# Per-sample mixed 3x3 convolution: the input scaling of pairs 2 to 15 is done by VectorE, ahead of its statistics of the next pair, instead of by ScalarE

## The chip, the core and the metric

The kernel runs on one core of one Trainium2 chip. The metric is the device time of one launch in microseconds (us), as the median of the runs shown.

## What is computed

The input x is a batch of 32 images of 64 channels and 56x56 pixels, float32. The reference, cut to what matters:

```python
xn = group_norm(x, G=32)                      # two channels share mean and variance
pooled = xn.mean(axis=(2, 3))                 # [32, 64]
a   = relu(pooled @ fc1_w.T + fc1_b)          # K = 4 hidden values per image
att = softmax(a @ fc2_w.T + fc2_b)            # 4 mixing weights per image
agg_w = einsum('bk,koihw->boihw', att, weight)  # an own 3x3 kernel for every image
agg_b = att @ bias
out = x + conv3x3(xn, agg_w, padding=1) + agg_b
```

So every image first needs its statistics, then its own mixture of four weight sets, and only then its convolution.

## The kernel before

**Tiles.** Two images make a pair (PAIRS = 16), 64 channels each on 64 of the 128 partitions; a pair's input is one tile `x` of 128x3136 float32 in a ring of four. The convolution is made of float16 products: the scaled input and the mixed weights are each split into a high and a low float16 part (`xh`, `xl`, `wh`, `wl`), and TensorE adds high x high, low weights x high inputs (`xh,wl`) and high weights x low inputs (`xl,wh`) in PSUM. Each pair has four groups g = 0 to 3 of 14 output rows, and in each group the three products take 36 matmuls each: nine taps for the two images and the two halves of a picture. Line numbers below are those of the kernel before.

**The stages of a pair p, and who does them.**
- VectorE (DVE) takes `bn_stats` of the input in seven chunks (L321), aggregates them and swaps neighbouring channels (L329, L333), and signals `s_mv`.
- GpSimd (POOL) makes the group statistics from them, seventeen instructions on 128x1 or 128x4 operands in a chain (`group_stats`, L281 to L297). Its sixteenth, L296, signals `s_sums`; its last, L297, signals `s_norm`: the scale `xsc` and the offset `xof` of the pair are then ready.
- TensorE (PE) waits for `s_sums` and sums over channels with two small matmuls (`image_sums`, L643, output `tiny`). From pair 2 on, the sums of pair p+2 stand in TensorE's program behind group 2 of pair p; the sums of pairs 2 and 3 stand in pair 1, those of pair 2 behind group 1's `xh,wl` products and those of pair 3 behind group 2.
- ScalarE (ACT) copies them to `hid` (L559); VectorE makes `logit` and its maximum `nmax` (`logits`, L378 to L382); ScalarE takes the exponential `ex` (L570); VectorE mixes the weights (`mixture`, from `exsum` in L386 over `mix` in L400 and L402 to L410).
- ScalarE scales the input in place (`normalise`, L520: x becomes x*xsc + xof, half a picture at a time, signalled by `s_xn`) and rounds it to `xh` (`high_inputs`, L527); VectorE subtracts to get `xl` (`low_inputs`, L455) and makes `wl` (L446); ScalarE makes `wh` (L541).
- `params` (L463 to L468) makes the scale and offset of the results, ScalarE applies them to PSUM (`results`, L581), and SyncE (SP) stores.

**Order.** Nothing is scheduled by a tool: each engine runs its own list in the order in which it is written, and semaphores tie the lists together. Up to pair 1 the order is written out step by step. After that VectorE's loop over p does, in this order, the statistics of pair p+2, then logits, mixture, low inputs, low weights and params of pair p+1, while TensorE convolves pair p. ScalarE's loop does the last results of pair p-1, then `hidden`, scaling, rounding and exponentials of pair p+1, then the results of pair p. SyncE's queue loads the input of pair p+4 once the low inputs of pair p are made.

Of the kernel before, what the change touches and what calls it, by code (L numbers as in the profile page):

```python
# [39 lines left out]
X_RING = 4  # L40
# [6 lines left out]
def dynamic_conv(nc, x, w_t, small, out):  # L47
    fp32, fp16 = mybir.dt.float32, mybir.dt.float16
    ACT, AX = mybir.ActivationFunctionType, mybir.AxisListType
# [5 lines left out]
    with ctx:  # L55
        def sb(name, shape, dt=fp32):
            return ctx.enter_context(nc.sbuf_tensor(name, shape, dt))
# [4 lines left out]
        def sem(name):  # L62
            return ctx.enter_context(nc.semaphore(name))


        x_sb = [sb(f"x{i}", [P, PIX]) for i in range(X_RING)]
# [46 lines left out]
        xsc = [sb(f"xsc{i}", [P, 1]) for i in range(2)]  # L113
        xof = [sb(f"xof{i}", [P, 1]) for i in range(2)]
# [27 lines left out]
        s_norm = sem("s_norm")  # L142
# [9 lines left out]
        s_xn = sem("s_xn")  # L152
# [9 lines left out]
        def rows_of(t, half):  # L162
            return t[:, half * HALF:(half + 1) * HALF]
# [141 lines left out]
        def _(dve):  # L305
            LINKS = 8

            def link(n, ins):
                ins.then_inc(dch, 1)
                dve.wait_ge(dch, n)  # L310
# [138 lines left out]
            def low_inputs(p, half):  # L449
# [3 lines left out]
                if p >= 2:  # L453
                    dve.wait_ge(s_conv, 2 * GROUPS * (p - 1))
                nc.vector.tensor_tensor(rows_of(xl[i], half), rows_of(x_sb[p % X_RING], half),  # L455
                                        rows_of(xh[i], half), ALU.subtract).then_inc(s_xl, 1)

            def params(p):
                n, i = LINKS * p, p % 2
                if p >= 2:  # L460

                    dve.wait_ge(s_res, 2 * GROUPS * (p - 1))
                nc.vector.tensor_scalar(par[i][:, 0:1], hid[:, RANGE:RANGE + 1], 1.0 / (WLIMIT * XSCALE), None,  # L463
                                        ALU.mult)
                nc.vector.reciprocal(rsum[:], exsum[:]).then_inc(dch, 1)
                link(n + 7, nc.vector.tensor_tensor(bprod[:], ex[:], small_sb[:, BIAS:BIAS + K], ALU.mult))
                link(n + 8, nc.vector.tensor_reduce(bsum[:], bprod[:], AX.X, ALU.add))
                nc.vector.tensor_scalar(par[i][:, 1:2], bsum[:], rsum[:], gm[i][:], ALU.mult,  # L468
                                        ALU.add).then_inc(s_par, 1)
# [23 lines left out]
            low_inputs(1, 0)  # L493
            low_inputs(1, 1)
            params(1)
            for p in range(1, PAIRS - 1):
                if p + 2 < PAIRS:
                    chunk_stats(p + 2)
                    channel_means(p + 2)
                logits(p + 1)  # L500
                mixture(p + 1)
                low_inputs(p + 1, 0)
                low_weights(p + 1)
                low_inputs(p + 1, 1)
                params(p + 1)


            i, n = last_pair % 2, GROUPS * PAIRS - 1
# [5 lines left out]
        @block.scalar  # L514
        def _(act):
            def normalise(p, half):
                i = p % 2
                act.wait_ge(s_norm, p + 1)
                v = rows_of(x_sb[p % X_RING], half)
                nc.scalar.activation(v, v, ACT.Identity, bias=xof[i][:], scale=xsc[i][:]).then_inc(s_xn, 1)  # L520

            def high_inputs(p, half):
                i = p % 2
                act.wait_ge(s_xn, 2 * p + half + 1)
                if p >= 2:
                    act.wait_ge(s_conv, 2 * GROUPS * (p - 1))
                nc.scalar.activation(rows_of(xh[i], half), rows_of(x_sb[p % X_RING], half),  # L527
                                     ACT.Copy).then_inc(s_xh, 1)

            def high_from_x(p, half):  # L530
                act.wait_ge(s_norm, p + 1)
                nc.scalar.activation(rows_of(xh[p], half), rows_of(x_sb[p], half), ACT.Identity,  # L532
                                     bias=xof[p][:], scale=xsc[p][:]).then_inc(s_xh, 1)

            def high_weights(p):
                i = p % 2
                act.wait_ge(s_mix, p + 1)
                act.wait_ge(s_wsc, p + 1)
                if p >= 2:
                    act.wait_ge(s_conv, 2 * GROUPS * (p - 1))  # L540
                nc.scalar.activation(wh[i][:], mix[:], ACT.Copy, scale=wsc[i][:]).then_inc(s_wh, 1)  # L541

            def first_high_weights(n):
                if n == 0:
                    act.wait_ge(s_mix, 1)
                    act.wait_ge(s_wsc, 1)
                else:
                    act.wait_ge(s_part, 2 * K)
                part = PARTS[n]
                nc.scalar.activation(wh[0][:, part], mix[:, part], ACT.Copy, scale=wsc[0][:]).then_inc(s_wh, 1)  # L550

            def hidden(p):
                act.wait_ge(s_fc1, 2 * (p + 1))
                if p >= 1:
                    act.wait_ge(s_par, p)

                columns = slice(0, K + 1) if p == 0 else slice(0, SUMS)
                for m in range(2):
                    nc.scalar.activation(hid[halves[m], columns], tiny[m][halves[m], columns],  # L559
                                         ACT.Copy).then_inc(s_hid, 1)  # L560

            def first_range():
                act.wait_ge(s_range, 2)
                for m in range(2):
                    nc.scalar.activation(hid[halves[m], RANGE:RANGE + 1], tiny[m][halves[m], RANGE:RANGE + 1],
                                         ACT.Copy).then_inc(s_hid, 1)

            def exponentials(p):
                act.wait_ge(s_logit, p + 1)
                nc.scalar.activation(ex[:], logit[:], ACT.Exp, bias=nmax[:]).then_inc(s_exp, 1)  # L570

            def results(p, g, images=range(2)):
                i, n = p % 2, GROUPS * p + g
                for m in images:
                    if g == 0:
                        if m == 0:
                            act.wait_ge(s_outp[i], 64 * (p // 2 + 1))
                        if p >= 2:
                            act.wait_ge(stored[i][m], 48 * (p // 2))
                    act.wait_ge(s_conv, 2 * n + m + 1)  # L580
                    nc.scalar.activation(o_sb[i][m][:, g * GN:(g + 1) * GN], acc[n % SLOTS][m][:, 0:GN], ACT.Identity,  # L581
                                         bias=out_par[i][m][:, 1:2], scale=out_par[i][m][:, 0:1]).then_inc(s_res, 1)

            act.dma_start(small_sb[:], small).then_inc(s_small, 16)
            act.wait_ge(s_warm, 1)
            nc.scalar.activation(warm[:], warm[:], ACT.Exp)
            hidden(0)
            exponentials(0)
            high_from_x(0, 0)
            first_range()  # L590
            high_from_x(0, 1)
            first_high_weights(0)
            act.wait_ge(s_xh, 2)
            normalise(0, 0)
            first_high_weights(1)
            normalise(0, 1)
            results(0, 0)
            hidden(1)
            results(0, 1, (0,))
            exponentials(1)  # L600
            results(0, 1, (1,))
            high_from_x(1, 0)
            high_from_x(1, 1)
            high_weights(1)
            results(0, 2)
            act.wait_ge(s_xh, 4)
            normalise(1, 0)
            normalise(1, 1)
            for p in range(1, PAIRS):
                results(p - 1, 3)  # L610
                if p + 1 < PAIRS:
                    hidden(p + 1)
                    normalise(p + 1, 0)
                    high_inputs(p + 1, 0)
                    normalise(p + 1, 1)
                    exponentials(p + 1)
                    high_inputs(p + 1, 1)
                    results(p, 0)
                    high_weights(p + 1)
                    results(p, 1)  # L620
                    results(p, 2)
                else:
                    for g in range(GROUPS - 1):
                        results(p, g)
                    results(p, GROUPS - 1, (0,))
                    act.wait_ge(s_res_last, 1)
                    for r in range(2):
                        first = r * HALF + BANDS[r][GROUPS - 1] * GN
                        act.dma_start(out_d[2 * p + 1, :, first:first + GN],
                                      o_sb[p % 2][1][halves[r], HALF - GN:HALF]).then_inc(stored[p % 2][1], 16)  # L630
# [151 lines left out]
```

## Time and profile before

| | before |
|---|---|
| median of 3 runs | 323.12 us (322.63 to 326.03) |
| the profiled execution | 323.93 us, its span 322.1 us |
| PE busy | 301.2 us (94% of the span) |
| DVE busy | 215.6 us (67%) |
| ACT busy | 198.2 us (62%) |
| POOL busy | 75.4 us (23%) |
| the chain that ended last | PE 82%, DVE 8%, POOL 4% |

The span runs from the first to the last instruction; the execution's own time is 1.8 us more. A row of the timeline gives a start and a duration in us, the engine, the line, the operation with output and inputs, how many instructions the row joins, and in brackets how long the engine sat idle before it and which instruction released it. Idle time on an engine that nobody waits for costs nothing.

### The profile page before, as it was taken

The page shows a single profiled execution, that of the slowest core. Times are in us where ns is not written, and L with a number is a line of the kernel's source. Part 1 is how long each engine was busy: PE and PEld are TensorE (multiplying, and loading weights), DVE is VectorE, ACT ScalarE, POOL GpSimd, SP SyncE. Part 2 cuts the span into 40 slices and gives each one's busy share as a digit, 9 for nine tenths or more (in the row PEclk, how much of TensorE's full clock was granted, in tenths as well). Part 3 has the DMA queues.
Part 4 walks back from the last instruction along what each step waited for, and adds up shares of the span by engine and source line. Part 5 has one row for each costly group of instructions (what it writes and reads, how often), then busy time and mean ns, then how long its engine had stood idle before and what let it go on. Part 6 is the DMA issues. An engine that isn't in the chain of part 4 may idle for free.

```text
span 322.1 us, 15578 instructions
## 1 busy us (share of the span) xinstructions
PE 301.2 (94%) x7038; PEld 265.2 (82%) x7038; DVE 215.6 (67%) x505; ACT 198.2 (62%) x260; POOL 75.4 (23%) x268
## 2 busy tenths in 40 slices
PE   7289877999899999999999999999999999999994
PEld 5157756988679999988999899967998799988883
DVE  2899584979569494948769494949678594719000
ACT  1090776786484849567684849486675849395321
POOL 1008266028310405040220404050311305000000
PEclk9769995999999999999999999999999999999999
DMA  7962306738392947648292947668392607051464
GB/s 260 421 268 65 141 2 150 254 86 286 77 275 93 228 177 176 227 112 288 51 258 111 239 166 184 218 136 273 84 293 56 180 2 205 2 147 60 118 171 119
DMA packets 16690, 53.61 MB, mean 166 GB/s; under 512 B 7280, under 2 KB 10352, under 8 KB 14704
## 3 DMA queue, kind: packets, MB, share of 16 engines
q1 hardware_dynamic: 16320, 52.40, 54.1%
q8 instruction: 55, 0.90, 1.1%
q10 hardware_dynamic: 304, 0.22, 0.3%
q14 instruction: 11, 0.09, 0.1%
HBM read 26.89 MB, written 25.69 MB: 163 GB/s over the span
## 4 chain that ended last, share of the span: by engine, by line
PE 82%; DVE 8%; POOL 4%; DMA 2%; issue 2%; ACT 0%; SPq 0%; POOLq 0%; DVEq 0%
PE acc L674 82%; DMA x<-x 2%; DVE stats L321 2%; DVE mix L402 2%; POOL var L285 1%; DVE wparts L337 1%; POOL vsum L281 1%; PE tiny L643 0%; DVE wl L446 0%; POOL root L286 0%; DVE mix L400 0%; DVE mv L329 0%; SPq L205 0%; POOL newton L287 0%; DVE o L511 0%
## 5 line engine op out<-in xcount | busy, mean ns | idle before, releaser
L581 ACT ACTIVATE o<-acc,out_par 128x392 f32<-128x392 f32 x127 | 78.9, 670 | 78.8 <-PE acc L674 78.4
L674 PE MATMUL acc<-xl,wh 64*64 64x385 f16 (+3 forms) x2304 | 119.8, 330 | 1.4 <-issue 1.4
L674 PE MATMUL acc<-xh,wh 64*64 64x385 f16 (+3 forms) x2304 | 118.1, 326 | 1.2 <-ACT wh L550 0.5
L674 PE MATMUL acc<-xh,wl 64*64 64x385 f16 (+3 forms) x2304 | 117.4, 325 | 0.6 <-issue 0.6
L674 PEld LDWEIGHTS acc<-xl,wh 64*64 64x64 f16 x2304 | 94.4, 109 | 11.4 <-issue 1.8
L674 PEld LDWEIGHTS acc<-xh,wl 64*64 64x64 f16 x2304 | 91.3, 107 | 11.3 <-issue 1.1
L674 PEld LDWEIGHTS acc<-xh,wh 64*64 64x64 f16 x2304 | 90.8, 108 | 11.9 <-ACT xh L532 0.9
L321 DVE BATCH_NORM_STATS2 stats<-x 128x6 f32<-128x448 f32 x112 | 60.8, 612 | 6.1 <-DMA x<-x 6.1
L455 DVE TENSOR_TENSOR xl<-x,xh 128x1568 f16<-128x1568 f32 x31 | 55.3, 1785 | 0.8 <-ACT x L520 0.8
L520 ACT ACTIVATE x<-x,xof,xsc 128x1568 f32<-128x1568 f32 x32 | 53.8, 1686 | 0.4
L527 ACT ACTIVATE xh<-x 128x1568 f16<-128x1568 f32 x28 | 42.0, 1502 | 0.4
L386 DVE TENSOR_REDUCE exsum<-ex 128x1 f32<-128x4 f32 x16 | 2.5, 156 | 58.2 <-ACT ex L570 58.2
L281 POOL TENSOR_TENSOR vsum<-mv,mv_other 128x1 f32<-128x1 f32 x15 | 4.3, 289 | 158.5 <-DVE mv_other L333 158.5
L402 DVE SCALAR_TENSOR_TENSOR mix<-w_sb,ex,mix 128x576 f32<-128x576 f32 (+2 forms) x51 | 40.0, 783 | 1.8
L541 ACT ACTIVATE wh<-mix,wsc 128x576 f16<-128x576 f32 x15 | 11.6, 776 | 19.6 <-DVE mix L410 19.6
L559 ACT ACTIVATE hid<-tiny 64x6 f32<-64x6 f32 (+1 forms) x32 | 5.3, 166 | 18.7 <-PE tiny L643 18.3
L643 PEld LDWEIGHTS tiny<-sums,ones 64*64 64x64 f32 x64 | 5.5, 142 | 13.2 <-DVE sums L364 7.6
L643 PE MATMUL tiny<-sums,ones 64*64 64x6 f32 (+1 forms) x64 | 5.2, 194 | 11.8 <-DVE sums L364 7.4
L511 DVE TENSOR_SCALAR o<-acc,out_par 128x392 f32<-128x392 f32 x1 | 0.7, 684 | 20.3 <-PE acc L674 20.3
L446 DVE SCALAR_TENSOR_TENSOR wl<-mix,wsc,wh 128x576 f16<-128x576 f32 x16 | 13.0, 811 | 0.0
L656 PE MATMUL acc<-ones 128*128 128x256 f16 x58 | 10.8, 368 | 1.1 <-POOL eye L237 1.1
L656 PEld LDWEIGHTS acc<-ones 128*128 128x128 f16 x58 | 7.3, 130 | 3.5 <-POOL eye L237 1.1
(71 smaller groups left out, 146.3 us busy)
## 6 DMA issues: line engine op xcount, KB each, us to landing
x<-x SPq DMA_DIRECT2D x15, 1568.0 KB, 9.8
out<-o SPq DMA_DIRECT2D x30, 392.0 KB, 4.5
out<-o SPq DMA_DIRECT2D x30, 294.0 KB, 4.1
out<-o SPq DMA_DIRECT2D x44, 98.0 KB, 2.8
w_sb<-w_t SPq DMA_DIRECT2D x2, 576.0 KB, 8.7
out_par<-par SPq DMA_DIRECT2D x64, 0.5 KB, 2.1
x<-x SPq DMA_DIRECT2D x1, 896.0 KB, 7.1
x<-x SPq DMA_DIRECT2D x1, 448.0 KB, 3.7
```

The source lines that it names most:

```text
L281: tt(vsum[:], mv[:, 1:2], mv_other[:, 1:2], ALU.add)
L321: ins = nc.vector.bn_stats(stats[:, t, :], x_sb[p % X_RING][:, t * CHUNK:(t + 1) * CHUNK])
L402: ins = nc.vector.scalar_tensor_tensor(**share, scalar=ex[:, k:k + 1], in1=mix[:, part], op0=ALU.mult, op1=ALU.add)
L446: nc.vector.scalar_tensor_tensor(out=wl[i][:], in0=mix[:], scalar=wsc[i][:], in1=wh[i][:], op0=ALU.mult, op1=ALU.subtract).then_inc(s_wl, 1)
L455: nc.vector.tensor_tensor(rows_of(xl[i], half), rows_of(x_sb[p % X_RING], half), rows_of(xh[i], half), ALU.subtract).then_inc(s_xl, 1)
L520: nc.scalar.activation(v, v, ACT.Identity, bias=xof[i][:], scale=xsc[i][:]).then_inc(s_xn, 1)
L527: nc.scalar.activation(rows_of(xh[i], half), rows_of(x_sb[p % X_RING], half), ACT.Copy).then_inc(s_xh, 1)
L541: nc.scalar.activation(wh[i][:], mix[:], ACT.Copy, scale=wsc[i][:]).then_inc(s_wh, 1)
L581: nc.scalar.activation(o_sb[i][m][:, g * GN:(g + 1) * GN], acc[n % SLOTS][m][:, 0:GN], ACT.Identity, bias=out_par[i][m][:, 1:2], scale=out ...
L643: nc.tensor.matmul(tiny[m][halves[m], columns], ones[halves[m], 0:C], sums[halves[m], columns], start=True, stop=True).then_inc(s_fc1, 1)
L656: nc.tensor.matmul(acc[SLOTS - 1][0][:, 0:2 * P], ones[:].bitcast(fp16)[:, 0:P], ones[:].bitcast(fp16), start=True, stop=True)
L674: ins = nc.tensor.matmul(pixels[:, top:bottom, left:right], weights[i][halves[m], tap * C:(tap + 1) * C], window, start=start and step == ...
```

## The change

VectorE gets a function `normalise` that does the same in-place scaling with `tensor_scalar`, and calls it at the head of its loop for pair p+1 (so for pairs 2 to 15), before the statistics of pair p+2. ScalarE's loop no longer does it; ScalarE still scales pairs 0 and 1.

```diff
--- before.py
+++ after.py
@@ -455,6 +455,12 @@
+            def normalise(p, half):
+                i = p % 2
+                dve.wait_ge(s_norm, p + 1)
+                v = rows_of(x_sb[p % X_RING], half)
+                nc.vector.tensor_scalar(v, v, xsc[i][:], xof[i][:], ALU.mult, ALU.add).then_inc(s_xn, 1)
+
             def params(p):
@@ -494,6 +500,8 @@
             for p in range(1, PAIRS - 1):
+                for half in range(2):
+                    normalise(p + 1, half)
                 if p + 2 < PAIRS:
                     chunk_stats(p + 2)
                     channel_means(p + 2)
@@ -514,10 +522,9 @@
             def normalise(p, half):
-                i = p % 2
                 act.wait_ge(s_norm, p + 1)
-                v = rows_of(x_sb[p % X_RING], half)
-                nc.scalar.activation(v, v, ACT.Identity, bias=xof[i][:], scale=xsc[i][:]).then_inc(s_xn, 1)
+                v = rows_of(x_sb[p], half)
+                nc.scalar.activation(v, v, ACT.Identity, bias=xof[p][:], scale=xsc[p][:]).then_inc(s_xn, 1)
@@ -610,9 +617,7 @@
                 if p + 1 < PAIRS:
                     hidden(p + 1)
-                    normalise(p + 1, 0)
                     high_inputs(p + 1, 0)
-                    normalise(p + 1, 1)
                     exponentials(p + 1)
                     high_inputs(p + 1, 1)
```

On VectorE, at the first pass of its loop (p = 1), between the params of pair 1 and the exponential sum of pair 2, the order before is:

```order
L468 TENSOR_SCALAR par1<-bsum,rsum,gm1 128x1
L321 BN_STATS stats<-x3 128x6 x7
L329 BN_AGGR mv<-stats 128x2
L333 STREAM_SHUFFLE mv_other<-mv 128x2
L378 SCALAR_TENSOR_TENSOR prod<-hid,small_sb 128x20
L381 TENSOR_REDUCE logit<-prod 128x4
L382 TENSOR_REDUCE nmax<-logit 128x1
L386 TENSOR_REDUCE exsum<-ex 128x1
```

and after the change, where L474 is the old L468 and L462 is the new scaling:

```order
L474 TENSOR_SCALAR par1<-bsum,rsum,gm1 128x1
L462 TENSOR_SCALAR x2<-x2,xsc0,xof0 128x1568 x2
L321 BN_STATS stats<-x3 128x6 x7
L329 BN_AGGR mv<-stats 128x2
L333 STREAM_SHUFFLE mv_other<-mv 128x2
L378 SCALAR_TENSOR_TENSOR prod<-hid,small_sb 128x20
L381 TENSOR_REDUCE logit<-prod 128x4
L382 TENSOR_REDUCE nmax<-logit 128x1
L386 TENSOR_REDUCE exsum<-ex 128x1
```

Two scalings of pair 2, which need `s_norm` of pair 2, now stand in front of the statistics of pair 3, and the logits of pair 2 behind both. The other thirteen passes change in the same way.

On ScalarE, at the same pass, after `hidden` of pair 2, the order before is:

```order
L559 ACTIVATE hid<-tiny1 64x6
L520 ACTIVATE x2<-x2,xof0,xsc0 128x1568
L527 ACTIVATE xh0<-x2 128x1568
L520 ACTIVATE x2<-x2,xof0,xsc0 128x1568
L570 ACTIVATE ex<-logit,nmax 128x4
L527 ACTIVATE xh0<-x2 128x1568
```

and after the change, with L566, L534 and L577 for the old L559, L527 and L570:

```order
L566 ACTIVATE hid<-tiny1 64x6
L534 ACTIVATE xh0<-x2 128x1568
L577 ACTIVATE ex<-logit,nmax 128x4
L534 ACTIVATE xh0<-x2 128x1568
```

The exponential of a pair now has one rounding ahead of it behind `hidden`, where it had two scalings and a rounding.

## Rows read from the trace of the kernel before

**Rows 1.** The page: shares of the chain that ended last, by engine.
```profile
PE 82%; DVE 8%; POOL 4%; DMA 2%; issue 2%; ACT 0%; SPq 0%; POOLq 0%; DVEq 0%
```

**Rows 2.** Windows: length, then busy us (instructions) of each engine, granted clock, DMA share, GB/s.
```profile
158.00:176.00 18.00, 18.00 (x448) 17.46 (x443) 13.33 (x31) 12.43 (x17) 4.03 (x17) 1.00 0.62 183
```

**Rows 3.** Waits of all engines: us in total, times, longest.
```profile
PE tiny L643 <- POOL sums L296: 4.5, 2, 3.7
PE acc L674 <- issue: 2.3, 3, 1.4
```

**Rows 4.** Groups of instructions by form: busy us, mean ns of one | idle before.
```profile
L520 ACT ACTIVATE x<-x,xof,xsc 128x1568 f32<-128x1568 f32 x32 | 53.8, 1686 | 0.4
...
L455 DVE TENSOR_TENSOR xl<-x,xh 128x1568 f16<-128x1568 f32 x31 | 55.3, 1785 | 0.8 <-ACT x L520 0.8
...
L400 DVE TENSOR_SCALAR mix<-w_sb,ex 128x576 f32<-128x576 f32 x15 | 7.5, 500 | 0.0
...
L400 DVE TENSOR_SCALAR mix<-w_sb,ex 128x256 f32<-128x256 f32 x1 | 0.3, 347 | 0.0
```

**Rows 5.** Timeline of POOL, 50 to 57 us: end of pair 2's chain, pair 3's.
```profile
50.48 0.26 POOL L297 TENSOR_SCALAR xof<-gm,rstd 128x1 f32<-128x1 f32 x1
51.95 0.19 POOL L281 TENSOR_TENSOR vsum<-mv,mv_other 128x1 f32<-128x1 f32 x1 [1.21 <-DVE mv_other L333]
...
56.55 0.19 POOL L296 TENSOR_TENSOR sums<-std,wpart 128x1 f32<-128x1 f32 x1
```

**Rows 6.** Timeline of VectorE, 47 to 65 us: the first pass of its loop.
```profile
47.52 3.77 DVE L321 BATCH_NORM_STATS2 stats<-x 128x6 f32<-128x448 f32 x7
...
52.20 0.16 DVE L382 TENSOR_REDUCE nmax<-logit 128x1 f32<-128x4 f32 x1
56.45 0.16 DVE L386 TENSOR_REDUCE exsum<-ex 128x1 f32<-128x4 f32 x1 [4.10 <-ACT ex L570]
...
57.04 0.50 DVE L400 TENSOR_SCALAR mix<-w_sb,ex 128x576 f32<-128x576 f32 x1
...
62.78 1.78 DVE L455 TENSOR_TENSOR xl<-x,xh 128x1568 f16<-128x1568 f32 x1
```

**Rows 7.** Timeline of VectorE at pair 1's exponential, where ScalarE is free.
```profile
35.88 0.16 DVE L386 TENSOR_REDUCE exsum<-ex 128x1 f32<-128x4 f32 x1 [0.36 <-ACT ex L570]
```

**Rows 8.** Timeline of TensorE, 50 to 61 us: the sums of pairs 2 and 3.
```profile
50.56 0.28 PE L643 MATMUL tiny<-sums,ones 64*64 64x6 f32 x2 [3.67 <-POOL sums L296]
...
56.12 1.76 PE L674 MATMUL acc<-xh,wh 64*64 64x392 f16 x36
57.61 1.76 PE L674 MATMUL acc<-xh,wl 64*64 64x392 f16 x36
...
60.70 0.23 PE L643 MATMUL tiny<-sums,ones 64*64 64x6 f32 x4
```

**Rows 9.** Windows around TensorE's wait at 46.9 us, columns as in rows 2.
```profile
49.00:50.00 1.00, 0.00 (x0) 0.00 (x0) 1.00 (x3) 0.00 (x0) 0.83 (x4) 0.50 0.04 1
...
55.00:56.00 1.00, 1.00 (x22) 0.94 (x18) 0.00 (x0) 1.00 (x1) 0.81 (x4) 0.62 1.05 284
```

**Rows 10.** Timeline of POOL, 69 to 79 us: the chain of pair 4.
```profile
69.60 0.19 POOL L281 TENSOR_TENSOR vsum<-mv,mv_other 128x1 f32<-128x1 f32 x1 [12.62 <-DVE mv_other L333]
...
75.71 1.89 POOL L295 TENSOR_SCALAR xsc<-rstd 128x1 f32<-128x1 f32 x1
77.57 0.73 POOL L296 TENSOR_TENSOR sums<-std,wpart 128x1 f32<-128x1 f32 x1
```

**Rows 11.** Timeline of VectorE beside it: the mixture and low inputs of pair 3.
```profile
72.43 0.50 DVE L400 TENSOR_SCALAR mix<-w_sb,ex 128x576 f32<-128x576 f32 x1
...
75.73 1.78 DVE L455 TENSOR_TENSOR xl<-x,xh 128x1568 f16<-128x1568 f32 x1
```

**Rows 12.** Timeline, 43 to 47 us: a POOL instruction beside VectorE's low inputs of pair 1.
```profile
43.41 3.50 DVE L455 TENSOR_TENSOR xl<-x,xh 128x1568 f16<-128x1568 f32 x2 [0.80 <-ACT x L520]
...
43.67 3.29 POOL L285 TENSOR_SCALAR var<-diff,vhalf 128x1 f32<-128x1 f32 x1
```

## The prediction, made before the changed kernel had run

> **What bounds the kernel now.** I read the chain of waits first: TensorE holds 82% of it, so VectorE and ScalarE matter only where TensorE waits for them [rows 1]. Then a window in the settled part: in 18 us TensorE is busy for all 18.00 at a granted clock of 1.00, VectorE for 13.33, ScalarE for 12.43 [rows 2]. Nothing that these two give or take there moves the end as long as they keep up. Then the list of waits. From the first full pair on TensorE's only waits for another engine are those for POOL's sums, 4.5 us in two, the longest 3.7; what else interrupts it is 2.3 us in three gaps with no releaser [rows 3]. Taking all of that "issue" time away would be worth 2.3 us. So there is next to nothing to win, and the question is whether the first passes, where the pipeline is still short, lose something.
>
> That is best asked at TensorE's sums. The sums of pair 2 end an idle time of 3.67 us, at 50.56; those of pair 3 are taken at 60.70 without a wait [rows 8]. POOL had these ready at 56.55 + 0.19 = 56.74 [rows 5]. The margin for pair 3 is therefore 60.70 - 56.74 = 3.96 us, and it is the smallest thing in the path of the change.
>
> **Settled pairs: no cost.** ScalarE loses 28 of its 32 in-place scalings, 28 x 1.686 = 47.2 us of 53.8 [rows 4]. It is not what TensorE waits for, so I put this at nothing. VectorE gains 28 `tensor_scalar` of 128x1568. Price of one: the same operation on `mix` takes 347 ns for 256 columns and 500 for 576, which is 0.478 ns a column, so 500 + 992 x 0.478 = 974 ns [rows 4]; a second scalar operand may add a little, so I take 1.0 us, 2.0 us for a pair. The upper bound is the rate of `xl`, 1.785 us for the same shape [rows 4], or 3.6 a pair; the lower one is 0.95. Two more us on VectorE in a pair make 13.33 + 2.0 = 15.3 of 18 [rows 2]. Its idle time in a pair is the some 4 us before `exsum` (4.10 in the first pass), where it waits for ScalarE's exponential behind two scalings and a rounding [rows 6]. Those scalings go, so the exponential comes earlier as well, and VectorE gets ahead of TensorE rather than behind. That idle time is the cover; without it a pair would be 2.0 us longer.
>
> SyncE's list is unchanged. Its loads wait for the low inputs of a pair whose buffer is read again four pairs later, so a shift of some us in them hides in the ring. POOL's list is unchanged too.
>
> **The first pass: a new wait.** VectorE's first scaling is that of pair 2 and needs POOL's `s_norm` of pair 2. That comes with L297, which ends at 50.48 + 0.26 = 50.74 [rows 5]. VectorE arrives there at 47.52, when it used to start the statistics of pair 3 [rows 6]. So it idles for 3.3 us, in front of work that could have been done, and everything behind is queued: the statistics of pair 3, the logits of pair 2 and its mixture. Step by step:
> - scaling of pair 2 from 50.8 to 52.8 (50.74 and a semaphore; 2 x 1.0);
> - statistics of pair 3 from 52.8 instead of 47.52. Before, POOL's first instruction on them came 51.95 - 47.52 = 4.43 us after their start [rows 5, 6]; now at T = 57.2 instead of 51.95;
> - logits of pair 2: `nmax` ended 52.36 - 47.52 = 4.84 us after the start of the statistics [rows 6], now at 57.65. ScalarE has long done `hidden` and the first rounding and stands at the exponential. Where ScalarE was free, `exsum` came 0.36 us after `nmax` [rows 7], so now at 58.0, instead of 56.45;
> - from there on the mixture and the low inputs keep their pace, 1.55 us later. The second `xl` of pair 2 ended at 62.78 + 1.78 = 64.56 [rows 6], now at 66.1.
>
> **What this does to POOL.** Undisturbed, POOL needs 56.74 - 51.95 = 4.79 us from its first instruction to L296 [rows 5]. Pair 3's sums would be ready at 57.2 + 4.8 = 62.0, already 1.3 us after TensorE asks for them. But POOL will not be undisturbed. Before, it ran inside VectorE's idle time of 4.10 us [rows 6]. Now `exsum` comes 0.8 us after POOL's start and the first `mix` 57.04 - 56.45 = 0.6 later [rows 6], at T + 1.4. What VectorE's large instructions do to POOL's tiny ones is in two places of the trace. One POOL instruction on a single column lasted 3.29 us, as long as two `xl` beside it [rows 12]. And in pair 4's chain POOL started at 69.60 and VectorE's `mix` at 72.43, 2.83 later; L295 then lasted 1.89 us beside an `xl` of 1.78 that had started in the same instant, and L296 ended at 78.30, 8.70 us after the start instead of 4.79 [rows 10, 11]. In that stretch about one POOL instruction passes for each VectorE instruction. The Trainium skill, "SBUF — State Buffer", section "Who interferes with whom", says that a VectorE instruction with two SBUF inputs or in a 2-port mode and a GpSimd instruction that reads SBUF exclude each other for a whole instruction; the trace agrees, with 3.29 us for such an instruction, where those of rows 5 take 0.19 to 0.26. By that rule the sums come late and the time is the forecast below; without it, the 1.3 us of the undisturbed chain would be all.
>
> Sixteen instructions to L296 in 4.79 us are 0.3 us each, so at T + 1.4 POOL is in its fifth or sixth and some ten are left, against eight of VectorE without a gap (four on `mix`, the residual, `xl`, `wl`, `xl`), which end at 66.1. I expect L296 some 0.5 us behind them, in front of or among the small params: 66.6. TensorE gets its sums at 66.7 instead of 60.70: **a stall of 6.0 us**. Bounds: 1.3 (POOL not held at all), and 66.1 + 10 x 0.3 - 60.7 = 8.4 if none of the ten passes before 66.1. With scalings of 1.785 each everything is 1.6 later.
>
> **The clock.** After the idle time that began at 46.9 the granted clock was at 0.50 in 49 to 50 and still partly so in 55 to 56, at a mean of 0.62 [rows 9]; that is the 1.2 GHz level against 2.4. The two products from 50.56 to 56.12 took 5.56 us; at the full clock one takes 57.61 - 56.12 = 1.49 [rows 8], two 2.98. The fallen clock cost 2.6 us after a wait of 3.67. A wait of 6.0 is longer, so I expect the same again: **2.6 us**, between 0 (it does not fall) and about 3.
>
> **Later passes.** TensorE's delay is a gift to the others. The second pass starts its scaling when pair 3's L297 is through, about 66.9, where VectorE is free as well (pair 1's params took 47.52 - 46.91 = 0.6 behind its `xl` [rows 6, 12], so 66.7): no wait. Pair 4's statistics end near 73. TensorE reaches the place of its sums twelve products of 1.49 after that of pair 3 [rows 8], which was 60.70 + 17.9 = 78.6 and is now 8.6 later, 87.2. Even a chain held as in rows 10 fits. From then on VectorE needs some 16 us a pair with its waits and TensorE 17.9, so it stays ahead.
>
> **Sum.** 6.0 + 2.6 = 8.6 us, against nothing gained. The profiled execution took 323.93 us with a span of 322.1; a like one would take 332.5 (span 330.7). The median of the runs lies 0.8 below the profiled one, so I say **331.7 us**, 2.7% slower.
>
> **Rivals.**
> - *POOL slips through.* The chain of pair 3 takes its undisturbed 4.8 us, TensorE stalls for 1.3, with no fall of the clock: 323.1 + 1.3 = 324.4, not slower by what can be told. The place is TensorE's sums in pair 1; it decides for this as long as L296 ends before 60.70 + 3.2 = 63.9, that is within 6.7 us of POOL's start. For it: if VectorE's instructions leave gaps wide enough, POOL's fit in, as they do in rows 5. Against it: rows 10 and 12 name exactly this neighbourhood. Chance 0.10.
> - *The stall without the clock:* 323.1 + 6.0 = 329.1. Against it is rows 9. Chance 0.06.
> - *Later still:* the scaling runs at the rate of `xl`, or POOL gets no turn between VectorE's instructions. The first is worth 1.6 us, the second 8.4 - 6.0 = 2.4: 333.3 to 335.7. Chance 0.13.
> - *VectorE becomes the bound.* If its exponential is not earlier, and POOL is held in each pair, T comes 2.0 us later in each, and the 8.7 us of rows 10 would end after TensorE's place: 1 to 2 us in each of some twelve pairs, on top of the first stall, 345 to 355. Against it: 15.3 of 18 and the earlier exponential. Chance 0.03.
> - *ScalarE's relief pays.* All gaps without a releaser vanish and no stall appears: 323.1 - 2.3 = 320.8, under 1%. Chance 0.01.
>
> The forecast has 0.67. The range of 327.5 to 335.5 takes in it, the stall without the clock, and most of the later case. About 1% is what a measurement of this kernel can tell from no change: faster by more 0.01, within it 0.10, slower 0.89.
>
> **What would show it.** In the profile after: VectorE idle for about 3.3 us before its first scaling, released by POOL's L297; scalings of about 1.0 us; POOL's first instruction for pair 3 near 57.2, and its L295 and L294 as long as the VectorE instructions beside them; TensorE waiting for the sums once more, about 6 us at 60.7, with the granted clock at 0.50 after it; then full windows of TensorE with VectorE near 15.3 of 18. I am wrong if the second wait for sums is under 3 us, if a third appears, or if windows past 100 us show TensorE less than full.

## The result

The changed kernel takes **331.14 us** (median of 4 runs, 330.45 to 332.22) against 322.99 us for the kernel before, run beside it (also 4 runs): ratio 1.0248, 95% interval 1.0206 to 1.0289. The profiled execution took 332.22 us with a span of 330.3 us. The prediction said 331.7 us, in a range of 327.5 to 335.5. Ratios here and below leave out executions that were over 1.5% slower than the fastest of the same kernel.

In the changed kernel VectorE's scaling is L462, ScalarE's exponential L577, TensorE's sums L648 and its products L679. POOL's lines keep their numbers.

The list of waits of the changed kernel first, as in rows 3:

```profile
PE tiny L648 <- POOL sums L296: 10.7, 3, 6.4
...
DVE x L462 <- POOL xof L297: 4.0, 2, 3.2
```

Waits for POOL's sums went from 4.5 us in two to 10.7 us in three, and the longest is now 6.4. VectorE, which never waited for POOL's last instruction before, does so for up to 3.2 us. Next VectorE's timeline in the first pass, the one that answers to [rows 6]:

```profile
50.65 2.10 DVE L462 TENSOR_SCALAR x<-x,xsc,xof 128x1568 f32<-128x1568 f32 x2 [3.18 <-POOL xof L297]
52.67 3.78 DVE L321 BATCH_NORM_STATS2 stats<-x 128x6 f32<-128x448 f32 x7
...
57.87 0.16 DVE L386 TENSOR_REDUCE exsum<-ex 128x1 f32<-128x4 f32 x1 [0.36 <-ACT ex L577]
...
58.46 0.50 DVE L400 TENSOR_SCALAR mix<-w_sb,ex 128x576 f32<-128x576 f32 x1
58.99 2.53 DVE L402 SCALAR_TENSOR_TENSOR mix<-w_sb,ex,mix 128x576 f32<-128x576 f32 x3
...
61.76 1.78 DVE L455 TENSOR_TENSOR xl<-x,xh 128x1568 f16<-128x1568 f32 x1
63.46 0.81 DVE L446 SCALAR_TENSOR_TENSOR wl<-mix,wsc,wh 128x576 f16<-128x576 f32 x1
64.19 1.78 DVE L455 TENSOR_TENSOR xl<-x,xh 128x1568 f16<-128x1568 f32 x1
```

and POOL's, the chain of pair 3, which answers to [rows 5]:

```profile
57.10 0.19 POOL L281 TENSOR_TENSOR vsum<-mv,mv_other 128x1 f32<-128x1 f32 x1 [6.49 <-DVE mv_other L333]
...
59.12 0.90 POOL L287 TENSOR_SCALAR newton<-root,var 128x1 f32<-128x1 f32 x1
...
60.80 0.77 POOL L289 TENSOR_TENSOR rstd<-root,newton 128x1 f32<-128x1 f32 x1
61.67 1.92 POOL L290 TENSOR_SCALAR pooled<-diff,rstd 128x1 f32<-128x1 f32 x1
63.69 2.37 POOL L291 TENSOR_SCALAR fc1p<-small_sb,pooled 128x4 f32<-128x4 f32 x1
66.14 0.20 POOL L292 TENSOR_TENSOR sums<-fc1p,b_part 128x4 f32<-128x4 f32 x1
...
66.99 0.19 POOL L296 TENSOR_TENSOR sums<-std,wpart 128x1 f32<-128x1 f32 x1
```

Read the two together. POOL starts 5.15 us later than before, and 0.77 us later the exponential is there. L290 starts at 61.67 beside the `xl` of 61.76 and ends with it. L291 starts at 63.69 inside `wl`, does not end when `wl` does, and comes out at 66.06 behind the second `xl`. The five instructions from L292 to L296 then take one microsecond. L296 ends at 67.18, 10.1 us after the start, where it took 4.79 undisturbed. TensorE's timeline:

```profile
67.24 0.27 PE L648 MATMUL tiny<-sums,ones 64*64 64x6 f32 x2 [6.37 <-POOL sums L296]
...
70.06 3.13 PE L679 MATMUL acc<-xh,wl 64*64 64x392 f16 x36
72.86 1.75 PE L679 MATMUL acc<-xl,wh 64*64 64x392 f16 x36
74.34 1.76 PE L679 MATMUL acc<-xh,wh 64*64 64x392 f16 x36
...
87.90 0.23 PE L648 MATMUL tiny<-sums,ones 64*64 64x6 f32 x4
```

The sums of pair 3 end a wait of 6.37 us; those of pair 4, at 87.90, end none. In windows (columns as in rows 2):

```profile
61.00:62.00 1.00, 0.00 (x0) 0.00 (x0) 0.96 (x3) 0.13 (x1) 0.90 (x2) 1.00 0.97 401
66.00:67.00 1.00, 0.00 (x0) 0.00 (x0) 0.59 (x5) 0.00 (x0) 0.83 (x6) 0.57 0.00 0
72.00:73.00 1.00, 1.00 (x18) 0.93 (x14) 1.00 (x3) 0.00 (x0) 0.00 (x0) 0.51 0.00 0
166.00:184.00 18.00, 18.00 (x448) 17.97 (x443) 15.25 (x32) 9.26 (x15) 7.47 (x18) 1.00 0.62 183
```

The granted clock is at 0.57 at the end of the wait and at 0.51 as late as 72 to 73. Group 3 of pair 1, from 67.25 to 74.34, takes 7.09 us for three products that take 1.43 us each there at the full clock: 2.8 us lost. In the settled window TensorE is as full as before, VectorE went from 13.33 to 15.25 of 18, ScalarE from 12.43 to 9.26, and POOL from 4.03 to 7.47, since its instructions now run beside VectorE's large ones there: the chain that starts at 165.66 takes 6.5 us to L296, and TensorE asks for the sums only at 178.3, 6 us after its end.

### The profile page after: what moved, and what is told of

Its sections match the earlier page's. It is cut to its first block, busy times and chain, and to the rows that moved or that the text cites. A ratio compares the mean times of both kernels' runs of the same rounds, so it can differ in the third digit from the quotient of the medians.

```text
span 330.3 us, 15578 instructions
## 1 busy us (share of the span) xinstructions
PE 304.7 (92%) x7038; PEld 273.8 (83%) x7038; DVE 244.8 (74%) x533; ACT 154.0 (47%) x232; POOL 104.8 (32%) x268
## 4 chain that ended last, share of the span: by engine, by line
PE 78%; DVE 9%; POOL 7%; DMA 2%; issue 2%; ACT 0%; SPq 0%; POOLq 0%; DVEq 0%
PE acc L679 78%; DVE stats L321 3%; DMA x<-x 2%; DVE mix L402 2%; POOL var L285 1%; POOL fc1p L291 1%; DVE wparts L337 1%; POOL pooled L290 1%; POOL vsum L281 1%; POOL root L286 1%; PE tiny L648 1%; POOL newton L287 0%; DVE wl L446 0%; DVE mv L329 0%; POOL rstd L289 0%
## 5 line engine op out<-in xcount | busy, mean ns | idle before, releaser
L679 PE MATMUL acc<-xl,wh 64*64 64x385 f16 (+3 forms) x2304 | 118.8, 331 | 0.7 <-issue 0.6
L679 PE MATMUL acc<-xh,wh 64*64 64x385 f16 (+3 forms) x2304 | 117.7, 329 | 0.9 <-ACT wh L557 0.5
L679 PE MATMUL acc<-xh,wl 64*64 64x385 f16 (+3 forms) x2304 | 117.0, 328 | 0.2 <-issue 0.2
L679 PEld LDWEIGHTS acc<-xl,wh 64*64 64x64 f16 x2304 | 95.8, 109 | 9.1 <-issue 1.5
L679 PEld LDWEIGHTS acc<-xh,wl 64*64 64x64 f16 x2304 | 93.4, 108 | 9.2 <-issue 1.0
L679 PEld LDWEIGHTS acc<-xh,wh 64*64 64x64 f16 x2304 | 93.0, 109 | 9.4 <-ACT xh L539 0.9
L281 POOL TENSOR_TENSOR vsum<-mv,mv_other 128x1 f32<-128x1 f32 x15 | 4.3, 289 | 139.4 <-DVE mv_other L333 139.4
L534 ACT ACTIVATE xh<-x 128x1568 f16<-128x1568 f32 x28 | 42.1, 1502 | 0.8 <-DVE x L462 0.5
L462 DVE TENSOR_SCALAR x<-x,xsc,xof 128x1568 f32<-128x1568 f32 x28 | 29.3, 1090 | 4.0 <-POOL xof L297 4.0
L648 PE MATMUL tiny<-sums,ones 64*64 64x6 f32 (+1 forms) x64 | 5.2, 199 | 17.9 <-POOL sums L296 10.7
L648 PEld LDWEIGHTS tiny<-sums,ones 64*64 64x64 f32 x64 | 5.2, 146 | 19.5 <-POOL sums L296 11.9
L378 DVE SCALAR_TENSOR_TENSOR prod<-hid,small_sb 128x20 f32<-128x20 f32 x16 | 2.8, 178 | 24.0 <-ACT hid L566 24.0
L297 POOL TENSOR_SCALAR xof<-gm,rstd 128x1 f32<-128x1 f32 x15 | 17.4, 1160 | 0.0
L566 ACT ACTIVATE hid<-tiny 64x6 f32<-64x6 f32 (+1 forms) x32 | 5.3, 166 | 18.4 <-PE tiny L648 18.0
```

The source lines that it names most:

```text
L281: tt(vsum[:], mv[:, 1:2], mv_other[:, 1:2], ALU.add)
L297: ts(xof[i][:], gm[i][:], -XSCALE, rstd[:], ALU.mult, ALU.mult).then_inc(s_norm, 1)
L462: nc.vector.tensor_scalar(v, v, xsc[i][:], xof[i][:], ALU.mult, ALU.add).then_inc(s_xn, 1)
L648: nc.tensor.matmul(tiny[m][halves[m], columns], ones[halves[m], 0:C], sums[halves[m], columns], start=True, stop=True).then_inc(s_fc1, 1)
L679: ins = nc.tensor.matmul(pixels[:, top:bottom, left:right], weights[i][halves[m], tap * C:(tap + 1) * C], window, start=start and step == ...
```

## The experiments

Every kernel was compared with the kernel before, run beside it; ratios carry 95% intervals. Clock figures are those of each profile's windows.

**Scaling on VectorE from pair 3 on (e1), and from pair 4 on (e2).** In both ScalarE's loop scales the pairs ahead of that again.

```diff
 for p in range(1, PAIRS - 1):
-    for half in range(2):
-        normalise(p + 1, half)
+    if p + 1 >= 3:               # e2: >= 4
+        for half in range(2):
+            normalise(p + 1, half)
```

> Pair 2 is scaled by ScalarE again, pairs 3 to 15 by VectorE. Theory (the loss is the first pass of VectorE's loop: its scaling waits for POOL's pair 2, and pair 3's chain on POOL is then held by the mixture): the 6.4 us wait at pair 3's sums is gone, but the same thing can happen once in the second pass, with less lateness. There the scaling of pair 3 (2.1 us) pushes POOL's start on pair 4 from 69.6 to about 71.7, the exponential follows it closely, and L296 ends about 10.1 us after the start as in the changed kernel, at 81.8, against TensorE's place at 78.5: a wait of about 3.3 us, with the clock falling or not: 326.3 to 328.9 us. Rival 'the time goes on VectorE in every pair' (28 scalings cost something each): 12/14 or 13/14 of the loss stays, 330.5. Rival 'only the first scaling's place matters': 323.0, no wait for sums in pair 2.

> Pairs 2 and 3 are scaled by ScalarE, pairs 4 to 15 by VectorE. Theory: VectorE has gained enough on TensorE by the third pass. POOL's start on pair 5 is near 87.1, L296 at the worst 10 us later, 97, against TensorE's place near 97: wait 0 to 0.5 us, time 323 to 323.5, the same as before although 24 of 28 scalings still run on VectorE. Rival 'a cost in every pair': 12/14 of 8.2 us stay, 330.

Measured: e1 326.79 us, ratio 1.0103 (1.0056 to 1.0150); e2 323.98 us, ratio 1.0011 (0.9973 to 1.0048). So 24 of the 28 scalings cost nothing that can be measured, and the rival of a cost in every pair is out. In e1 the loss moved to the second pass, as its VectorE, POOL and TensorE rows show, in this order:

```profile
72.55 0.16 DVE L386 TENSOR_REDUCE exsum<-ex 128x1 f32<-128x4 f32 x1 [0.36 <-ACT ex L579]
```
```profile
71.79 0.19 POOL L281 TENSOR_TENSOR vsum<-mv,mv_other 128x1 f32<-128x1 f32 x1 [14.52 <-DVE mv_other L333]
...
81.69 0.19 POOL L296 TENSOR_TENSOR sums<-std,wpart 128x1 f32<-128x1 f32 x1
```
```profile
81.93 0.28 PE L654 MATMUL tiny<-sums,ones 64*64 64x6 f32 x2 [3.82 <-POOL sums L296]
```

POOL starts, the exponential is 0.76 us behind it, and L296 comes 10.1 us after the start: the same picture without any wait of VectorE for `s_norm` in front of it. The clock falls behind this wait too: the three products after it take 5.94 us instead of 4.28. The profile of e2 shows that this place has no slack even with ScalarE's scaling:

```profile
80.53 0.23 PE L654 MATMUL tiny<-sums,ones 64*64 64x6 f32 x2 [2.11 <-POOL sums L296]
```

In the kernel before, L296 of pair 4 ended at 78.30, just as TensorE came [rows 10]; here it ended 2 us later and TensorE waited. What it is worth is inside the spread between executions of the same kernel.

**Is POOL held, or only late? (e3)**

```diff
     logits(p + 1)
+    if p == 1:
+        dve.wait_ge(s_sums, 5)
     mixture(p + 1)
```

> The changed kernel with one wait more: in the first pass VectorE starts the mixture of pair 2 only when POOL has signalled the sums of pair 3. Theory (POOL is held by VectorE's large instructions): POOL's chain takes 4.8 us instead of 10.1, L296 at 61.9, TensorE waits 1.3 us for it instead of 6.4 and the clock stays up; the mixture comes 3.6 us later, its second low input at about 70, so TensorE waits another 2.2 to 2.5 us in pair 2 behind its first product. Sum 3.5 to 4 us: 326.5 to 327.0, faster than the changed kernel by some 4.5 us. Rival 'POOL was late only, not held': the added wait can only cost; as slow as the changed kernel or slower, 331 to 334.

Measured: 333.42 us, ratio 1.0331 (1.0294 to 1.0367). The number is that of the rival, the rows are those of the theory. POOL first, then TensorE:

```profile
57.35 0.19 POOL L281 TENSOR_TENSOR vsum<-mv,mv_other 128x1 f32<-128x1 f32 x1 [6.49 <-DVE mv_other L333]
...
61.98 0.19 POOL L296 TENSOR_TENSOR sums<-std,wpart 128x1 f32<-128x1 f32 x1
```
```profile
62.22 0.22 PE L650 MATMUL tiny<-sums,ones 64*64 64x6 f32 x2 [0.87 <-POOL sums L296]
...
68.26 1.69 PE L681 MATMUL acc<-xh,wh 64*64 64x392 f16 x36 [1.46 <-ACT o L590]
70.45 1.69 PE L681 MATMUL acc<-xh,wl 64*64 64x392 f16 x36 [0.50 <-DVE xl L455]
...
87.50 0.28 PE L650 MATMUL tiny<-sums,ones 64*64 64x6 f32 x2 [4.89 <-POOL sums L296]
```

With VectorE quiet, POOL's chain takes 4.82 us instead of 10.08, and the wait at pair 3's sums is 0.87 us. So POOL was held; that is shown. What my expectation missed is the last row: the same collision comes back at pair 4's sums for 4.89 us, with the clock falling behind it. The waits add up to 0.87 + 1.46 + 0.50 + 4.89 = 7.7 us, more than the 6.37 of the changed kernel. So e3 is as slow as the rival said, but not for the rival's reason.

**TensorE asks later (e4).**

```diff
-                if g == 2:
+                if g == 3:
                     image_sums(3)
```

> The changed kernel, with TensorE's sums of pair 3 behind group 3 of pair 1 instead of behind group 2. Nothing on VectorE, ScalarE's list or POOL moves. Theory: L296 still ends at 67.2, TensorE now gets there at 60.55 + 4.4 = 65.0, waits 2.2 us, no fall of the clock: 323.0 + 2.2 = 325.2. Rival 'TensorE waits for something else too (low inputs, results)': the time stays above 328.

Measured: 328.35 us, ratio 1.0167 (1.0136 to 1.0198), 3 us more than expected and inside what the rival said:

```profile
60.97 1.62 PE L679 MATMUL acc<-xh,wh 64*64 64x392 f16 x36 [1.01 <-ACT o L588]
...
67.66 0.28 PE L648 MATMUL tiny<-sums,ones 64*64 64x6 f32 x4 [2.22 <-POOL sums L296]
...
84.48 0.28 PE L648 MATMUL tiny<-sums,ones 64*64 64x6 f32 x2 [3.06 <-POOL sums L296]
```

The 2.22 us at pair 3 are as foreseen. The 1.01 us in front are a wait for a PSUM bank, which the rival had in mind and which the old stall had hidden; the larger part, 3.06 us, comes at pair 4 again. e3 and e4 tell the same thing. While VectorE does not have to wait for TensorE, its pass takes 16.8 us (statistics at 52.67 and 69.47 in the changed kernel, with 0.36 us of waiting for the exponential and 0.80 for `s_norm` in it) and TensorE's 17.8 (60.70 to 78.52 in the kernel before). It gains only 1.0 us a pass, and L296 lands 14.5 us behind the start of each pass's statistics (52.67 to 67.18; in e1 67.35 to 81.88). A lateness of 6.5 us at pair 3 is still 5.5 at pair 4 unless TensorE has been delayed meanwhile. The long stall of the changed kernel is also what ends the trouble: after it VectorE waits for `hid` of pair 3, which ScalarE makes behind TensorE's delayed results, and in that idle time POOL's chain of pair 4, from 73.91 on, runs free.

```profile
76.18 0.18 DVE L378 SCALAR_TENSOR_TENSOR prod<-hid,small_sb 128x20 f32<-128x20 f32 x1 [2.35 <-ACT hid L566]
```

**The scaling behind the statistics (e5).**

```diff
 for p in range(1, PAIRS - 1):
-    for half in range(2):
-        normalise(p + 1, half)
     if p + 2 < PAIRS:
         chunk_stats(p + 2)
         channel_means(p + 2)
+    for half in range(2):
+        normalise(p + 1, half)
```

> VectorE scales all the pairs of the changed kernel, but behind the statistics of the next pair and in front of the logits. The same work on every engine, only no wait for POOL in front of the statistics. Theory (half of the lateness is the 3.2 us wait for s_norm, the rest POOL being held): POOL starts pair 3 at 52.0 again, is held for 2.1 us by the scaling, then by the mixture from about 55.6; L296 at about 64.0 against TensorE's place at 60.6: a wait of 3.4 us, the clock falling (2.6) or not: 326.4 to 329.0 us. Rival 'the wait for s_norm is the whole cause': no wait for sums, 323.0. Rival 'only the amount of work on VectorE counts': as the changed kernel, 331.

Measured: 326.76 us, ratio 1.0118 (1.0066 to 1.0171), as the theory had it. The place in the list is worth about half of the loss (1.2% against 2.5%); what remains is POOL being held, now by the scaling too:

```profile
51.41 0.96 POOL L281 TENSOR_TENSOR vsum<-mv,mv_other 128x1 f32<-128x1 f32 x1 [1.21 <-DVE mv_other L333]
52.33 1.15 POOL L282 TENSOR_TENSOR diff<-mv,mv_other 128x1 f32<-128x1 f32 x1
```
```profile
63.57 0.28 PE L648 MATMUL tiny<-sums,ones 64*64 64x6 f32 x2 [4.16 <-POOL sums L296]
```

Two instructions of 0.19 us take 0.96 and 1.15 beside two scalings of 1.05. TensorE waits 4.16 us, not 3.4, and the clock falls behind it, at a cost of 1.7 us.

**The clock by itself (e6).**

```diff
                 if g == 2:
+                    slot_free(1, 3)
+                    keep_warm(50, (GROUPS + 3) % SLOTS)
                     image_sums(3)
```

> The changed kernel with 50 products of 128x256 on TensorE in front of the sums of pair 3, into a free PSUM bank that group 3 of pair 1 overwrites afterwards; they fill about 5.4 us of the wait of 6.4. Theory (2.6 us of the loss are the clock that falls in the wait): the sums still come at about 67.2, the clock stays at 1.00, 331.1 - 2.6 = 328.5 us. Rival 'the clock costs nothing of its own': 331.

Measured: 328.43 us, ratio 1.0155 (1.0097 to 1.0214).

```profile
60.81 5.63 PE L661 MATMUL acc<-ones 128*128 128x256 f16 x50 [0.68 <-ACT o L588]
67.48 0.22 PE L648 MATMUL tiny<-sums,ones 64*64 64x6 f32 x2 [1.04 <-POOL sums L296]
```
```profile
66.00:68.00 2.00, 0.96 (x23) 0.67 (x24) 1.13 (x7) 0.00 (x0) 1.49 (x7) 1.00 0.00 0
```

The sums come no earlier, the clock stays at 1.00, and 2.7 us are back (3.0 by the ratios). That the fall of the clock costs time of its own is thereby shown; its size only roughly, since the two intervals leave 2.3 us to either side.

**Can the idea be used where it helps? (v1, v2, v4, v5)** Only pair 2 is scaled by VectorE, and its statistics keep their place; the lists of ScalarE and TensorE are changed around the head, starting from the kernel before.

```diff
 # VectorE, first pass
                 logits(p + 1)
+                if p == 1:
+                    normalise(2, 0)
+                    normalise(2, 1)
                 mixture(p + 1)
 # ScalarE, first pass
+                    hidden(2)
+                    results(1, 0)
+                    exponentials(2)
+                    high_inputs(2, 0)
+                    high_inputs(2, 1)
+                    results(1, 1)
+                    high_weights(2)
+                    results(1, 2)
 # TensorE, pair 1
-            image_sums(2)
             pe.wait_ge(s_xl, 4)
             for g in range(2):
                 low_of_inputs(1, g)
+            image_sums(2)
 # TensorE, image_sums(3): behind group 0 of pair 2 instead of group 2 of pair 1
```

> From the kernel before: only pair 2 is scaled by VectorE, between its logits and its mixture; ScalarE makes the first results of pair 1 and the exponential of pair 2 ahead of the rounding; TensorE takes the sums of pair 2 behind the low inputs of pair 1's first two groups, and the sums of pair 3 behind group 0 of pair 2. Pairs 3 on as before. Theory (TensorE is the bound and each us of it that the head loses stays lost): the wait of 3.67 us and the 2.6 us of fallen clock at pair 2's sums go, VectorE's second low input of pair 2 ends at 62.8 instead of 64.6, TensorE waits about 1.7 us for it in pair 2; net 3.7 us less than before: 319.3 us. Rival 'the wait only moves' (POOL held again, low inputs later than worked out): 322 to 325.

> The kernel of v1_head again, in more rounds. Its profile showed the waits at the sums of pairs 2 and 3 gone and 1.4 us for the low inputs of pair 2, with a span 5.1 us shorter than before. Theory: 1.0 to 1.5% faster than before, ratio 0.985 to 0.990. Rival 'the gain of 0.9% was drift between runs': 0.995 to 1.0.

Measured: 320.60 us, ratio 0.9913 (0.9877 to 0.9950), and in the second set 320.16 us, ratio 0.9904 (0.9868 to 0.9940): **0.9% faster than the kernel before**, and 3.3% faster than the changed one by the quotient of the ratios. The first set's TensorE and ScalarE rows:

```profile
50.73 0.23 PE L661 MATMUL tiny<-sums,ones 64*64 64x6 f32 x2 [0.41 <-POOL sums L296]
...
62.70 1.69 PE L692 MATMUL acc<-xh,wl 64*64 64x392 f16 x36 [1.40 <-DVE xl L455]
```
```profile
52.62 0.29 ACT L579 ACTIVATE ex<-logit,nmax 128x4 f32<-128x4 f32 x1
```

The 3.67 us wait of [rows 8] is down to 0.41, and the exponential of pair 2 comes at 52.62. The profile of the second set has a wait of 2.09 us at pair 5's sums, which the first had not; this may be why less than the expected 3.7 us was gained, but that was not tested. The second set stayed just outside its expected 0.985 to 0.990, and the rival of mere drift, 0.995 to 1.0, is out by its interval.

v2 adds to v1 that TensorE does two products of groups 0 and 1 of pair 2 ahead of their low-input products, with the sums of pair 3 behind those.

> As v1_head, and TensorE does the first two products of groups 0 and 1 of pair 2 ahead of both low-input products, with the sums of pair 3 behind those. Theory: the 1.7 us wait for the low inputs is filled too, 317.6 to 318 us, if pair 3's low inputs (about 79.5) still meet TensorE (79.0). Rival as for v1_head: 321 to 325.

Measured: 322.36 us, ratio 0.9965 (0.9932 to 0.9998), in the range of the rival. The 1.40 us wait was filled, but POOL may not start pair 4's chain before TensorE has taken pair 3's sums: its list of waits has `POOL vsum L281 <- PE tiny L661`, 5.1 us, and TensorE pays 0.57, 2.87 and 1.41 us later on, with the clock at 0.50 in 76 to 78.

v4 keeps TensorE's sums of pair 2 behind the low inputs and nothing else of v1. v5 is v1 with ScalarE scaling pair 2; its exponential thereby stands behind two scalings and a rounding again, where v1 has it in front of both roundings.

> The kernel before with one thing of v1_head alone: TensorE takes the sums of pair 2 behind the low inputs of groups 0 and 1 of pair 1. ScalarE scales everything. Theory: the wait of 3.67 us is filled with work, but TensorE then reaches group 3 of pair 1 at 55.1 and stands for a bank until ScalarE's first results of pair 1 at 59.1, 4 us; pair 2 starts at 63.5 instead of 65.0: 321.6 us if the clock stays up, 324 if it falls. Rival 'the order on TensorE was the whole gain of v1_head': 319 us.

> The kernel of v1_head with ScalarE scaling pair 2 again. Theory (at this one place VectorE's scaling is worth something, since ScalarE stands in front of the exponential): exponential at 57.4 instead of 52.6, the low inputs of pair 2 end 3.2 us later than in v1_head, at 65.8, and TensorE waits there by as much: 320.6 + 3.2 = 323 to 324 us. Rival 'the order of results and sums alone makes the gain': 320.6.

Measured: v4 323.10 us, ratio 1.0000 (0.9968 to 1.0031); v5 325.32 us, ratio 1.0048 (1.0022 to 1.0074).

```profile
56.58 0.28 PE L643 MATMUL tiny<-sums,ones 64*64 64x6 f32 x4 [1.47 <-POOL sums L296]
58.81 3.01 PE L674 MATMUL acc<-xh,wh 64*64 64x392 f16 x36 [1.95 <-ACT o L581]
```
```profile
62.16 3.08 PE L691 MATMUL acc<-xh,wh 64*64 64x392 f16 x36 [2.69 <-ACT wh L547]
```

In v4 (first fence) the wait moves to a PSUM bank and the clock falls behind it (3.01 us for a product). In v5 (second fence) TensorE waits 2.69 us for `wh` of pair 2, and again the product behind it takes 3.08 us. Against v1 that is 1.4% by the ratios, 4.6 us where 3.2 were expected. The rows give 3.2, though in another way: 1.6 us more of waiting than in v1 (2.69 and 0.33 against 1.40), and 1.6 for the fall of the clock, which the expectation had left out. So TensorE's new place for the sums gains nothing alone, and v1's new lists without VectorE's scaling of pair 2 are slower than the kernel before. Two things were not run: VectorE's scaling with the old lists, and v1's lists with ScalarE scaling pair 2 behind the exponential. So it is not shown how much of the gain is the scaling's and how much comes from the exponential being earlier.

## Why the prediction was right, step by step

- **What bounds it.** Right: settled windows of 18 us have TensorE busy for 17.4 to 18.00 in both kernels, what is missing being gaps without a releaser, and e2 shows the scalings free from pair 4 on. Nothing was gained by relieving ScalarE, although it fell from 62% to 47% of the span.
- **The price of a scaling.** 1.0 us was said, 1.09 us measured, below; VectorE's 15.3 of 18 came out as 15.25.

```profile
L462 DVE TENSOR_SCALAR x<-x,xsc,xof 128x1568 f32<-128x1568 f32 x28 | 29.3, 1090 | 4.0 <-POOL xof L297 4.0
```

- **The new wait for `s_norm`.** 3.3 us said, 3.18 measured, and everything behind it within 0.2 us of the working: POOL's start 57.2 against 57.10, `exsum` 58.0 against 57.87, the second `xl` 66.1 against 65.97.
- **POOL held.** L296 at 66.6 said, 67.18 measured; the wait 6.0 against 6.37. Shown by e3, where the chain takes 4.82 us once VectorE is quiet. The detail was off: I let about one POOL instruction pass for each of VectorE's, but only five of the ten did, and the other five ran behind the last `xl`. So the long ones were L287 to L291, and L294 and L295, which I had named as the sign, took 0.26 and 0.23 us.
- **The clock.** 2.6 said, 2.8 in the trace and 2.7 by e6. That it would fall was argued from a row; that it would cost so much again was in part luck. Behind one and the same wait, the 3.67 us at pair 2's sums, the two products cost 2.6 us more than at the full clock in the kernel before, 2.7 in the changed one and 2.9 in e3, but 1.7 in e1, e2, e5 and e6 and 1.4 in e4.
- **The sum.** 8.6 said, 6.37 + 2.8 = 9.2 by these rows; the spans differ by 8.2. Two terms that were each a little small were offset: TensorE's gaps without a releaser were 2.3 us before [rows 3] and are 0.8 now. They come and go between profiles, so that the total came out within 0.6 us of the forecast is in part luck.
- **The margin.** The prediction called the 3.96 us at pair 3's sums the smallest thing in the path. It was not: in the kernel before, pair 4's sums were ready at 78.30 and taken at 78.52, a margin of 0.2 us, and e1, in which pair 3's sums end no wait, lost its time there.
- **Later passes.** Right for the changed kernel, for the reason given (TensorE's delay is a gift), though VectorE did wait 0.80 us for pair 3's `s_norm`, where no wait was said. But I had not seen how much hung on it: e3 and e4, which cut the first stall, got it back one pair later. The rival "VectorE becomes the bound" did not happen, but VectorE regains only 1.0 us a pass.
- **The rival on the other side**, POOL slipping through, would have needed a chain of at most 6.7 us; it took 10.1.
- **The sign "if a third appears".** The list has three waits for sums, 0.67, 3.67 and 6.37 us. The first, at pair 1's sums, was there before (0.82 us) and was not counted; from pair 2's on there are two, as said.

## What to carry to other kernels

Before moving work to an idle engine, look at the first passes, where the distance between producer and consumer is shortest: work that waits for a late result should not stand in front of work that is ready. Idle time of one engine can be the time in which another gets its turn; count what small dependent chains run inside it before filling it. And when a stall is cut in a pipeline that is just keeping up, ask what its delay had been healing: the wait may come back one stage later.

## What the runs showed of the hardware that was not expected

- **A held POOL instruction can miss its turn.** Rows 12 show one instruction of 3.29 us across two `xl` of 1.78; in the changed kernel L291 took 2.37 us across the end of a `wl` and a whole `xl`, where L285 and L291 take 0.26 and 0.30 undisturbed. The same 2.37 us for L291 are in e1, e4, e5 and v1. The Trainium skill, "SBUF — State Buffer", section "Who interferes with whom", has whoever issues first hold the shared ports for its whole instruction. L290's 1.92 us beside one `xl` of 1.78 agree; these two rows show a longer hold, and the measurement decides.
- **The clock does not fall after a fixed wait.** In the kernel before it was at 0.50 in 49 to 50 for a wait that began at 46.9 [rows 9]. In the changed kernel a wait from 60.9 on left it at 1.00 in 61 to 62 and it was at 0.57 only in 66 to 67. In v4 two waits of 1.47 and 1.95 us close together brought it down, and in v5 one of 2.69; in e4 one of 2.22 us did not. A fall cost between 1.4 us (pair 2's sums in e4) and 2.9 us (the same place in e3).
